# Wide self-attention: the next pair's scores directly behind the turns, ahead of reciprocals and values, and the probabilities copied ahead of the maxima

## The chip, the cores and the metric

The kernel runs on one NeuronCore of a Trainium2 chip. The time is the device time of one launch in microseconds (us). TensorE (PE in the rows) does the matmuls and transposes, VectorE (DVE), ScalarE (ACT) and GpSimd (POOL) the rest; PEld is the loading of TensorE's stationary operand. The engines run their own instruction lists in order and meet at semaphores.

## What is computed

The program is a decoder of six sub-layers on x of 16 batches x 256 rows x 128 columns. The change touches one of them, the self-attention of the second layer (16 heads of width 32), and only in the order of its instructions:

```python
def _mha(x, y, ...):                                  # here y = x, causal = True
    xn = _ln(x, lnx_g, lnx_b)
    yn = _ln(y, lny_g, lny_b)
    q = einsum('bsc,hcd->bhsd', xn, wq)
    k = einsum('btc,hcd->bhtd', yn, wk)
    v = einsum('btc,hcd->bhtd', yn, wv)
    a = softmax(einsum('bhsd,bhtd->bhst', q, k) * D ** (-0.5), axis=-1)
    a = a * mask                                      # masked after the softmax
    o = einsum('bhst,bhtd->bhsd', a, v)
    x_out = x + o.transpose(0, 2, 1, 3).reshape(...) @ li1_w + li1_b
```

## The kernel before

All stages run one after another. `attend_self` is called twice: with heads of width 8 (tiles `s2s_`) and with heads of width 32 (`WIDE`, tiles `s5a_`). It goes through 16 batches t of 8 steps p; a step handles a pair of heads. There is no scheduler and no pool: the order on every engine is the order in which the Python loops are written, and the semaphores only delay.

For a pair p of a batch, the work is a chain over three engines:

- TensorE `scores(p)`: q k^T into `scoreP[p % 2]` (L2269).
- VectorE `maxes(p)`: the row maxima, negated, into `nmax` (L2353).
- ScalarE `exps(p)`: four exponentials with row sums, into `prob[p % 2]` and `den` (L2181).
- TensorE `turn(p)`: six transposes of the probabilities into `probP` (L2279).
- VectorE `turn_out(p)`: mask and copy to `probT` (L2364).
- TensorE `pv(quad)`: after two pairs, probabilities times values into `oP` (L2299).

Between these go "items", all through one PSUM tile, `itemP`, which each must find free: `T` (transposed normalized rows, L2234), `Q0`, `Q1` (L2237), `K0`, `K1` (L2240) and `V0`, `V1` (L2244) of the projections, which ScalarE takes out; `R0`, `R1` (the transposed reciprocals of the softmax sums of the batch before, L2249) and `L` (its output projection, L2253), which VectorE takes out (L2385 for R, L2378 for L). TensorE's side of an item is called `make`, the other engine's side `take`. The tables say in which step an item is made: at place A `V0, V1, Q1, K1, L, T, Q0, K0` in steps 0 to 7, at place B `R0` in step 1 and `R1` in step 2. Since `itemP` is one tile, `make` waits for the `take` of the item before it: `Q1` for `R0`, `K1` for `R1`, and `T` for `L`:

```python
before = {"V0": [("K0", b + 1)], "V1": [("V0", b + 1)], "R0": [("V1", cap(b + 2)), ("L", b)],
          "Q1": [("R0", b), ("V1", b + 1)], "R1": [("Q1", cap(b + 2)), ("R0", b + 1)],
          "K1": [("R1", b), ("Q1", b + 1)], "L": [("K1", cap(b + 2)), ("R1", b + 1)],
          "T": [("L", b - 1), ("K1", b)], "Q0": [("T", b + 1)], "K0": [("Q0", b + 1)]}[n]
```

ScalarE takes a step's item ahead of that step's exponentials. `LEAD` is true in the narrow call only; there the scores of a pair already stand one step ahead.

Of the kernel before, what the change touches and what calls it, by code (L numbers as in the profile page):

```python
# [26 lines left out]
def wait(eng, sem, value):  # L27

    if isinstance(value, int) and value <= 0:
        return  # L30
    eng.wait_ge(sem, value)
# [1879 lines left out]
def attend_self(nc, ident, dram, tag, hat, base, dst, kind, D, ln, bias, src, affine=None, twice=False):  # L1911
# [6 lines left out]
    WIDE = D == 32  # L1918
# [10 lines left out]
    with ExitStack() as ctx:  # L1929
# [47 lines left out]
        def batches(eng):  # L1977
            for j in range(NB // 2):
                for s in range(2):
                    yield 2 * j + s, s  # L1980

        def first(t):
            return isinstance(t, int) and t == 0

        def last(t):
            return isinstance(t, int) and t == NB - 1
# [19 lines left out]
        LEAD = not WIDE  # L2006

        def following(t, s, p):
            if p + 1 < PAIRS:
                return t, s, p + 1  # L2010
            return None if last(t) else (t + 1, 1 - s, 0)

        def at(table, t, s, p, doing):
            for n, d in table.get(p, []):
                if (d < 0 and first(t)) or (d > 0 and last(t)):
                    continue
                doing(n, t + d, s if d == 0 else 1 - s)
# [9 lines left out]
        @block.sync  # L2027
        def _(sp):
            prep.load(sp)
            load_all(sp, S["loaded"], loads)  # L2030
# [184 lines left out]
        def _(pe):  # L2215
# [40 lines left out]
            def scores(t, s, p):  # L2256
                i = p % 2
                c = p // 2
                if p == 0:
                    pe.wait_ge(used["Q0"], t + 1)  # L2260
                    pe.wait_ge(used["K0"], t + 1)
                if p == 4:
                    pe.wait_ge(used["Q1"], t + 1)
                    pe.wait_ge(used["K1"], t + 1)
                wait(pe, S["maxed"] if kind == "causal" else S["exped"], t * PAIRS + p - 1)
                rows_of = lambda h: slice(64 * (p % 2) + 32 * h, 64 * (p % 2) + 32 * h + 32)
                for r, (a, b) in enumerate(CUTS):
                    for h in range(2):
                        ins = nc.tensor.matmul(scoreP[i][:, h, a:b], q[rows_of(h), c, r * P:r * P + P], k[rows_of(h), c, 0:b - a],  # L2269
                                               start=True, stop=True)  # L2270
                ins.then_inc(S["scores"], 1)

            def turn(t, s, p):
                i = p % 2
                pe.wait_ge(S["exped"], t * PAIRS + p + 1)
                wait(pe, S["probT_ready"], t * PAIRS + p)
                for h in range(2):
                    for m, a in enumerate(BLOCKS):
                        ins = nc.tensor.transpose(probP[:, h, m * P:m * P + P], prob[i][:, h, a:a + P], ident[:])  # L2279
                ins.then_inc(S["turned"], 1)  # L2280
# [29 lines left out]
            for n in ("T", "Q0", "K0", "V0") if LEAD else ("T", "Q0", "K0"):  # L2310
                if n != "T":
                    pe.wait_ge(used["T"], 1)
                make(n, 0, 0)
            if LEAD:
                scores(0, 0, 0)
            if bias:
                pe.wait_ge(S["bo_ready"], 1)
            for t, s in batches(pe):
                for p in range(PAIRS):
                    new = following(t, s, p) if LEAD else (t, s, p)  # L2320
                    if new:
                        scores(*new)
                    at(AT_A, t, s, p, make)
                    e = earlier(t, s, p, 1)
                    if e:
                        turn(*e)
                    at(AT_B, t, s, p, make)
                    e = earlier(t, s, p, 2)
                    if e and e[2] % 2 == 1:
                        pv(e[0], e[1], e[2] // 2)  # L2330
# [5 lines left out]
        @block.vector  # L2336
        def _(ve):
            st = Steps(ve, S["step"])
            st.begin(0)
            ve.wait_ge(S["masks"], 2)  # L2340

            def maxes(t, s, p):
                i = p % 2
                n = t * PAIRS + p
                ve.wait_ge(S["scores"], n + 1)
                wait(ve, S["exped"], n - 2 if kind == "causal" else n - 3)
                if kind == "causal":
                    for r, (a, b) in enumerate(CUTS):
                        for h in range(2):
                            ins = nc.vector.tensor_tensor_reduce(low[n % 3][:, h, a:b], scoreP[i][:, h, a:b], mask[:, a:b], -1.0, BIG, ALU.add,  # L2350
                                                                 ALU.min, nmax[:, p % 4, h, r:r + 1])
                else:
                    ins = nc.vector.tensor_reduce(nmax[:, p % 4, :, :].rearrange("p h r -> p (h r)"),  # L2353
                                                  scoreP[i][:].rearrange("p h (r k) -> p (h r) k", r=2), AX_X, ALU.max, negate=True)
                ins.then_inc(S["maxed"], 1)

            def turn_out(t, s, p):
                i = p % 4
                ve.wait_ge(S["turned"], t * PAIRS + p + 1)
                wait(ve, S["pv"], t * QUADS + p // 2 - 1)  # L2360
                if kind == "causal":
                    nc.vector.tensor_copy(probT[i][:], probP[:, :, 0:3 * P]).then_inc(S["probT_ready"], 1)  # L2362
                else:
                    nc.vector.tensor_tensor(probT[i][:], probP[:, :, 0:3 * P], mask[:].unsqueeze(1).to_broadcast([P, 2, 3 * P]),  # L2364
                                            ALU.mult).then_inc(S["probT_ready"], 1)

            def recip(t, s):
                ve.wait_ge(S["exped"], t * PAIRS + PAIRS)
                wait(ve, S["expanded"], t)
                nc.vector.reciprocal(rden[:], den[s][:]).then_inc(S["recip"], 1)  # L2370

            def take(n, b, s):
                if n not in ("L", "R0", "R1"):
                    return
                ve.wait_ge(made[n], b + 1)
                if n == "L":
                    ve.wait_ge(S["carried"], b + 1)
                    nc.vector.tensor_tensor(rows(dst, b), rows(dst, b), itemP[:, 0:TB * P].rearrange("p (g c) -> p g c", g=TB),  # L2378
                                            ALU.add).then_inc(used["L"], 1)
                    return  # L2380
                wait(ve, made["L"], b)
                half = int(n[1])
                ve.wait_ge(S["o_out"], b * 4 + 2 * half + 2 if WIDE else b + 1)
                w = 2 if WIDE else 1
                nc.vector.tensor_tensor(oT[:, w * half:w * half + w, :], oU[:, w * half:w * half + w, :],  # L2385
                                        itemP[:, 0:w * L].rearrange("p (c l) -> p c l", c=w), ALU.mult).then_inc(used[n], 1)

            if affine:
                prep.stats(ve, st, 0, 0)
            prep.stats(ve, st, 0, 1)  # L2390
            if affine:
                prep.stats(ve, st, 1, 0)
            ve.wait_ge(S["loaded"], LOADED)
            if bias:
                ve.wait_ge(S["values_out"], 1)
                nc.vector.tensor_tensor(bo[:], bo[:], oP[:, 0, 0:C], ALU.add).then_inc(S["bo_ready"], 1)
                ve.wait_ge(S["bo_ready"], 1)
            if LEAD:
                maxes(0, 0, 0)
            for t, s in batches(ve):  # L2400
                st.begin(t)
                for p in range(PAIRS):
                    new = following(t, s, p) if LEAD else (t, s, p)
                    if new:
                        maxes(*new)
                    if p == 0 and not first(t):
                        recip(t - 1, 1 - s)
                    e = earlier(t, s, p, 1)
                    if e:
                        turn_out(*e)  # L2410
                    at(AT_A, t, s, p, take)
                    at(AT_B, t, s, p, take)
                    if p == 0 and not last(t):
                        prep.stats(ve, st, t + 1, 1)
                    if p == 3 and affine and t + 2 < NB:
                        prep.stats(ve, st, t + 2, 0)
            turn_out(NB - 1, 1, PAIRS - 1)
            recip(NB - 1, 1)
            for n in (("R0", "R1", "L") if WIDE else ("R0", "L")):
                take(n, NB - 1, 1)  # L2420
            ve.wait_ge(used["L"], NB)
# [1543 lines left out]
```

## Time and profile before

| | |
|---|---|
| time before, median of 3 runs (lowest to highest) | 2798.28 us (2797.87 to 2806.37) |
| the profiled execution: its time, its span | 2795.5 us, 2793.8 us |
| mean granted TensorE clock over the span | 0.924 |
| busy over the span: PE, PEld, DVE, ACT, POOL | 86%, 64%, 72%, 59%, 40% |
| the changed stage (s5a) in the trace | scores from 1716.3 us, last probabilities at about 2160 us |
| scores(0) to scores(0) of the next batch | 27.51 us |

The profiled execution is one run, 2.8 us below the median. Its time is the span and 1.7 us around it. Shares of the whole span mix stages with different limits; for this change only the rows of the stretch 1716 to 2163 us count.

### The profile page before, as it was taken

What the parts mean: (1) busy time and instruction counts of PE and PEld (TensorE: products, weight loads), DVE (VectorE), ACT (ScalarE), POOL (GpSimd) and SP (SyncE); (2) the same over time, 40 slices, a digit from 0 to 9 for tenths busy, and PEclk for the clock granted to TensorE, in tenths of its full rate; (3) what the DMA queues carried; (4) which work ended last, traced back from release to release, by engine and by line L of the source; (5) the groups of instructions that cost most, each with busy time, mean ns of one, the idle gap of its engine ahead of it and who ended that gap; (6) DMA issues with size and microseconds to landing.
All of it is one profiled execution on the core that took longest, in us unless ns stands there. A gap on an engine that the chain in (4) does not pass through costs nothing. (4 is left out here: it accounts for less than half of the span.)

```text
span 2793.8 us, 48818 instructions
## 1 busy us (share of the span) xinstructions
PE 2405.5 (86%) x16107; PEld 1793.3 (64%) x16107; DVE 2002.1 (72%) x4456; ACT 1641.1 (59%) x4541; POOL 1108.5 (40%) x1577
## 2 busy tenths in 40 slices
PE   5888888887987999979974997999999789998696
PEld 4666666666974666656642774666666567765585
DVE  6999999996335777758979463777776557767565
ACT  6777767772225888866654344777776256654211
POOL 4455785865641111112321312222220155522774
PEclk7999999989997999999986998999999889999798
DMA  8500000004750000000004000000000000000376
GB/s 333 231 1 1 7 10 5 12 7 135 223 159 33 2 2 2 2 16 1 2 1 68 7 1 19 2 1 2 2 1 1 27 1 1 1 1 15 102 225 198
DMA packets 74187, 129.80 MB, mean 46 GB/s; under 512 B 29129, under 2 KB 47633, under 8 KB 69842
## 3 DMA queue, kind: packets, MB, share of 16 engines
q1 hardware_dynamic: 62418, 103.46, 12.3%
q0 software_dynamic: 9216, 19.02, 1.9%
q10 hardware_dynamic: 2304, 4.20, 0.4%
q8 instruction: 132, 2.16, 0.3%
q14 instruction: 117, 0.96, 0.1%
HBM read 69.23 MB, written 57.41 MB: 45 GB/s over the span
## 5 line engine op out<-in xcount | busy, mean ns | idle before, releaser
L1218 DVE TENSOR_TENSOR_SCAN s_state<-s_decay,s_state 128x4096 f32<-128x4096 f32 x32 | 279.0, 8718 | 1.6
L1090 PE MATMUL s_ysumP<-s_state,ident 128*128 128x256 f32 x1024 | 253.6, 395 | 0.0
L2181 ACT ACTIVATE s5a_prob<-s5a_scoreP,s5a_nmax 128x256 f32<-128x256 f32 x512 | 235.5, 481 | 22.7 <-DVE s5a_nmax L2353 21.0
L930 ACT ACTIVATE s_decay<-s_delta,s_aneg 128x255 f32<-128x255 f32 x512 | 211.8, 495 | 53.2 <-POOL s_delta L756 53.0
L2181 ACT ACTIVATE s2s_prob<-s2s_low,s2s_nmax 128x128 f32<-128x128 f32 (+1 forms) x512 | 225.4, 448 | 1.6 <-DVE s2s_nmax L2350 1.6
L1090 PEld LDWEIGHTS s_ysumP<-s_state,ident 128*128 128x128 f32 x1024 | 199.1, 201 | 27.6
L2353 DVE TENSOR_REDUCE s5a_nmax<-s5a_scoreP 128x4 f32<-128x1024 f32 x128 | 156.1, 1220 | 67.3 <-PE s5a_scoreP L2269 65.1
L2350 DVE CUSTOM_DVE_ANT_0 s2s_low<-s2s_scoreP,s2s_mask 128x128 f32<-128x128 f32 (+1 forms) x512 | 151.8, 353 | 55.6 <-PE s2s_scoreP L2269 54.3
L997 PE MATMUL s_bcP<-s_bc,s_sel 96*128 96x256 bf16 x768 | 131.6, 309 | 67.5 <-DVE s_state L1228 49.0
L2364 DVE TENSOR_TENSOR s5a_probT<-s5a_probP,s5a_mask 128x768 f32<-128x768 f32 x128 | 122.5, 957 | 63.1 <-PE s5a_probP L2279 62.0
L1228 DVE TENSOR_TENSOR s_state<-s_state,s_bcP 128x1024 f32<-128x1024 f32 x128 | 149.2, 1215 | 17.5 <-PE s_bcP L997 15.4
L1206 DVE TENSOR_TENSOR s_state<-s_bcP,s_du 128x1024 f32<-128x1024 f32 x128 | 146.6, 1213 | 10.6 <-POOL s_du L759 10.2
L997 PEld LDWEIGHTS s_bcP<-s_bc,s_sel 96*128 96x128 bf16 x768 | 78.6, 109 | 111.5 <-DVE s_state L1228 61.4
L2362 DVE COPY s2s_probT<-s2s_probP 128x768 f32<-128x768 f32 x128 | 122.3, 955 | 36.8 <-PE s2s_probP L2279 36.8
L2269 PE MATMUL s5a_scoreP<-s5a_k,s5a_q 32*128 32x256 f32 x1024 | 147.2, 405 | 0.8 <-ACT s5a_k L2160 0.8
L744 POOL TENSOR_TENSOR s_lost<-s_em,s_part 128x512 f32<-128x512 f32 x16 | 127.1, 7942 | 39.2 <-ACT s_part L910 39.2
L2269 PE MATMUL s2s_scoreP<-s2s_k,s2s_q 32*128 32x128 f32 (+1 forms) x1024 | 120.1, 356 | 4.8 <-issue 4.8
L2279 PE MATMUL s2s_probP<-ident,s2s_prob 128*128 128x128 f32 x768 | 110.1, 280 | 12.3 <-DVE s2s_probT L2362 5.9
L2279 PEld LDWEIGHTS s2s_probP<-ident,s2s_prob 128*128 128x128 f32 x768 | 87.7, 143 | 40.4 <-ACT s2s_prob L2181 31.8
L2279 PEld LDWEIGHTS s5a_probP<-ident,s5a_prob 128*128 128x128 f32 x768 | 89.4, 142 | 32.8 <-ACT s5a_prob L2181 19.8
L2181 ACT ACTIVATION_READ_ACCUMULATOR s5a_prob<-s5a_scoreP,s5a_nmax 128x1 f32 x512 | 110.2, 215 | 0.0
L2269 PEld LDWEIGHTS s5a_scoreP<-s5a_k,s5a_q 32*128 32x128 f32 x1024 | 88.7, 187 | 32.6 <-issue 26.1
(674 smaller groups left out, 6320.8 us busy)
## 6 DMA issues: line engine op xcount, KB each, us to landing
sorted<-blank SPq DMA_DIRECT2D x32, 1105.0 KB, 27.9
s_state<-in_m_w SPq DMA_DIRECT2D x40, 512.0 KB, 4.2
s5n_m_w<-in_m_w SPq DMA_DIRECT2D x40, 384.0 KB, 3.8
s_decay<-sorted SPq DMA_DIRECT2D x40, 130.0 KB, 2.6
s5n_m_xin<-sorted SPq DMA_DIRECT2D x40, 130.0 KB, 3.2
s4w_mats<-s_scratch SPq DMA_DIRECT2D x4, 1024.0 KB, 13.1
s_state<-parts SPq DMA_DIRECT2D x8, 256.0 KB, 6.7
s_state<-parts ACTq DMA_DIRECT2D x8, 256.0 KB, 7.1
```

The costliest lines, as they stand in the source:

```text
L744: st.do(nc.gpsimd.tensor_tensor(lost[:], em[:], part[:], ALU.subtract))
L930: ins = nc.scalar.activation(decay[c][:, n, 1:], delta[:, c, 1:], ACT.Exp, scale=aneg[:, c, n:n + 1])
L997: ins = nc.tensor.matmul(bcP[k % 2][:, n, :], sel[:, line + n, :], bc3[s][:], start=True, stop=True)
L1090: ins = nc.tensor.matmul(ysumP[:, c, :], ident[:], state[s][:, c, n, :], start=False, stop=(n == NS - 1))
L1206: ins = nc.vector.tensor_tensor(state[s][:, c, GN * g:GN * g + GN, :], bcP[g % 2][:], du[:, c:c + 1, :].to_broadcast([P, GN, L]), ALU.mult)
L1218: nc.vector.tensor_tensor_scan(cells, flat(decay[c]), cells, 0.0, ALU.mult, ALU.add).then_inc(S["scanned"], 1)
L1228: nc.vector.tensor_tensor(part, part, bcP[k % 2][:], ALU.mult).then_inc(S["bc_used"], 1)
L2181: ins = nc.scalar.activation(prob[i][:, h, a:b], (low[n % 3] if kind == "causal" else scoreP[i])[:, h, a:b], ACT.Exp, bias=nmax[:, p % 4, ...
L2269: ins = nc.tensor.matmul(scoreP[i][:, h, a:b], q[rows_of(h), c, r * P:r * P + P], k[rows_of(h), c, 0:b - a], start=True, stop=True)
L2279: ins = nc.tensor.transpose(probP[:, h, m * P:m * P + P], prob[i][:, h, a:a + P], ident[:])
L2350: ins = nc.vector.tensor_tensor_reduce(low[n % 3][:, h, a:b], scoreP[i][:, h, a:b], mask[:, a:b], -1.0, BIG, ALU.add, ALU.min, nmax[:, p % ...
L2353: ins = nc.vector.tensor_reduce(nmax[:, p % 4, :, :].rearrange("p h r -> p (h r)"), scoreP[i][:].rearrange("p h (r k) -> p (h r) k", r=2), ...
```

## The change

In the wide call alone, on TensorE `scores(p + 1)` is issued in step p directly behind `turn(p - 1)`; before, it was issued at the start of step p + 1, behind place B (`R0`, `R1`) and behind `pv`. On VectorE `maxes(p + 1)` is issued directly behind `turn_out(p - 1)`; before, it stood behind the takes of `R0`, `R1`, `L` and behind the statistics of the next batches. The first pair's scores and maxima are issued ahead of the loop. ScalarE's, GpSimd's and the DMA queues' lists are not changed, and the narrow call keeps its order. No instruction is added or removed.

```diff
@@ TensorE
-            if LEAD:
-                scores(0, 0, 0)
+            scores(0, 0, 0)
...
                 for p in range(PAIRS):
-                    new = following(t, s, p) if LEAD else (t, s, p)
-                    if new:
+                    new = following(t, s, p)
+                    if not WIDE and new:
                         scores(*new)
                     at(AT_A, t, s, p, make)
                     e = earlier(t, s, p, 1)
                     if e:
                         turn(*e)
+                    if WIDE and new:
+                        scores(*new)
                     at(AT_B, t, s, p, make)
@@ VectorE
-            if LEAD:
-                maxes(0, 0, 0)
+            maxes(0, 0, 0)
...
                 for p in range(PAIRS):
-                    new = following(t, s, p) if LEAD else (t, s, p)
-                    if new:
+                    new = following(t, s, p)
+                    if not WIDE and new:
                         maxes(*new)
                     if p == 0 and not first(t):
                         recip(t - 1, 1 - s)
                     e = earlier(t, s, p, 1)
                     if e:
                         turn_out(*e)
+                    if WIDE and new:
+                        maxes(*new)
                     at(AT_A, t, s, p, take)
                     at(AT_B, t, s, p, take)
```

The first place is on TensorE, in a batch from the second on, from `turn(0)` in step 1 to the item `K1` in step 3. Before (L2279 turn, L2249 R0 and R1, the two rows of L2299 one pv, L2269 scores, L2237 Q1, L2240 K1):

```order
L2279 MATMUL s5a_probP<-ident,s5a_prob 128x128 x6
L2249 MATMUL s5a_itemP<-ident,s5a_rdx 128x128 x4
L2299 MATMUL s5a_oP<-s5a_probT,s5a_v 32x256 x4
L2299 MATMUL s5a_oP<-s5a_probT,s5a_v 32x128 x4
L2269 MATMUL s5a_scoreP<-s5a_k,s5a_q 128x256 x4
L2237 MATMUL s5a_itemP<-s5a_xqT,s5a_wq 128x256 x2
L2279 MATMUL s5a_probP<-ident,s5a_prob 128x128 x6
L2249 MATMUL s5a_itemP<-ident,s5a_rdx 128x128 x4
L2269 MATMUL s5a_scoreP<-s5a_k,s5a_q 128x256 x4
L2240 MATMUL s5a_itemP<-s5a_xkT,s5a_wk 128x256 x2
```

Now, the same stretch of TensorE's list in the changed kernel:

```order
L2279 MATMUL s5a_probP<-ident,s5a_prob 128x128 x6
L2269 MATMUL s5a_scoreP<-s5a_k,s5a_q 128x256 x4
L2249 MATMUL s5a_itemP<-ident,s5a_rdx 128x128 x4
L2299 MATMUL s5a_oP<-s5a_probT,s5a_v 32x256 x4
L2299 MATMUL s5a_oP<-s5a_probT,s5a_v 32x128 x4
L2237 MATMUL s5a_itemP<-s5a_xqT,s5a_wq 128x256 x2
L2279 MATMUL s5a_probP<-ident,s5a_prob 128x128 x6
L2269 MATMUL s5a_scoreP<-s5a_k,s5a_q 128x256 x4
L2249 MATMUL s5a_itemP<-ident,s5a_rdx 128x128 x4
L2240 MATMUL s5a_itemP<-s5a_xkT,s5a_wk 128x256 x2
```

The scores moved ahead of `R0` and `pv`, and ahead of `R1`; nothing else moved, and each item still stands directly ahead of the next turn. So `R0` and `R1` now stand directly, or with one pv between, ahead of the item that waits for their take.

The second place is on VectorE, in the same batch, from `turn_out(0)` in step 1 to the take of `L` in step 4. Before (turn_out, take of R0, maxima; turn_out, take of R1, maxima; turn_out, statistics, maxima; turn_out, take of L):

```order
L2364 TENSOR_TENSOR s5a_probT<-s5a_probP,s5a_mask 128x768
L2385 TENSOR_TENSOR s5a_oT<-s5a_oU,s5a_itemP 128x512
L2353 TENSOR_REDUCE s5a_nmax<-s5a_scoreP 128x4
L2364 TENSOR_TENSOR s5a_probT<-s5a_probP,s5a_mask 128x768
L2385 TENSOR_TENSOR s5a_oT<-s5a_oU,s5a_itemP 128x512
L2353 TENSOR_REDUCE s5a_nmax<-s5a_scoreP 128x4
L2364 TENSOR_TENSOR s5a_probT<-s5a_probP,s5a_mask 128x768
L1858 BN_STATS s5a_n_stat<-xres 128x6 x2
L1861 BN_AGGR s5a_n_stat<-s5a_n_stat 128x2 x2
L2353 TENSOR_REDUCE s5a_nmax<-s5a_scoreP 128x4
L2364 TENSOR_TENSOR s5a_probT<-s5a_probP,s5a_mask 128x768
L2378 TENSOR_TENSOR s_xo<-s_xo,s5a_itemP 128x256
```

Now, from the maxima behind `turn_out(0)` on (the lines are one higher in the changed file):

```order
L2354 TENSOR_REDUCE s5a_nmax<-s5a_scoreP 128x4
L2386 TENSOR_TENSOR s5a_oT<-s5a_oU,s5a_itemP 128x512
L2365 TENSOR_TENSOR s5a_probT<-s5a_probP,s5a_mask 128x768
L2354 TENSOR_REDUCE s5a_nmax<-s5a_scoreP 128x4
L2386 TENSOR_TENSOR s5a_oT<-s5a_oU,s5a_itemP 128x512
L2365 TENSOR_TENSOR s5a_probT<-s5a_probP,s5a_mask 128x768
L2354 TENSOR_REDUCE s5a_nmax<-s5a_scoreP 128x4
L1858 BN_STATS s5a_n_stat<-xres 128x6 x2
L1861 BN_AGGR s5a_n_stat<-s5a_n_stat 128x2 x2
L2365 TENSOR_TENSOR s5a_probT<-s5a_probP,s5a_mask 128x768
L2354 TENSOR_REDUCE s5a_nmax<-s5a_scoreP 128x4
L2379 TENSOR_TENSOR s_xo<-s_xo,s5a_itemP 128x256
```

Each of the three takes (R0, R1, L) stood directly behind a turn_out and now stands behind the maxima of the pair after, which wait for that pair's scores.

## Rows read from the trace of the kernel before

**Rows 1.** Windows, whole stage and two batches: busy us by engine, then granted clock

```profile
core 0: us, PE busy (x) PEld busy (x) DVE busy (x) ACT busy (x) POOL busy (x), PEclk, DMA share, GB/s
...
1716.00:2163.00 447.00, 435.39 (x3523) 299.45 (x3524) 322.28 (x434) 348.49 (x1274) 108.27 (x247) 0.98 0.01 1
1806.00:1862.00 56.00, 55.23 (x463) 38.05 (x461) 41.59 (x58) 44.76 (x166) 15.55 (x36) 1.00 0.00 1
```

**Rows 2.** Timeline of PE, one batch: start us, length us, line, operation, count [idle before]

```profile
1914.83 0.82 PE L2279 MATMUL s5a_probP<-ident,s5a_prob 128*128 128x128 f32 x6
1915.68 0.66 PE L2249 MATMUL s5a_itemP<-ident,s5a_rdx 128*128 128x128 f32 x4
1916.27 0.86 PE L2299 MATMUL s5a_oP<-s5a_probT,s5a_v 128*32 128x256 f32 x16
1917.06 1.13 PE L2269 MATMUL s5a_scoreP<-s5a_k,s5a_q 32*128 32x256 f32 x8
1918.12 1.13 PE L2237 MATMUL s5a_itemP<-s5a_xqT,s5a_wq 128*128 128x256 f32 x4
1919.09 0.82 PE L2279 MATMUL s5a_probP<-ident,s5a_prob 128*128 128x128 f32 x6
...
1921.59 1.13 PE L2240 MATMUL s5a_itemP<-s5a_xkT,s5a_wk 128*128 128x256 f32 x4
...
1925.16 2.05 PE L2253 MATMUL s5a_itemP<-s5a_wo,s5a_oT 128*128 128x128 f32 x16
1927.04 0.82 PE L2279 MATMUL s5a_probP<-ident,s5a_prob 128*128 128x128 f32 x6
1927.79 1.13 PE L2269 MATMUL s5a_scoreP<-s5a_k,s5a_q 32*128 32x256 f32 x8
1929.24 0.44 PE L2234 MATMUL s5a_itemP<-ident,s5a_hs 128*128 128x128 f32 x2 [0.32 <-DVE s_xo L2378]
1929.51 0.82 PE L2279 MATMUL s5a_probP<-ident,s5a_prob 128*128 128x128 f32 x6
...
1942.34 0.82 PE L2279 MATMUL s5a_probP<-ident,s5a_prob 128*128 128x128 f32 x6
```

**Rows 3.** Timeline of DVE in the same batch

```profile
1911.21 1.22 DVE L2353 TENSOR_REDUCE s5a_nmax<-s5a_scoreP 128x4 f32<-128x1024 f32 x1 [0.90 <-PE s5a_scoreP L2269]
1912.35 0.34 DVE L2370 RECIPROCAL s5a_rden<-s5a_den 128x32 f32<-128x32 f32 x1
...
1918.23 1.22 DVE L2353 TENSOR_REDUCE s5a_nmax<-s5a_scoreP 128x4 f32<-128x1024 f32 x1 [1.00 <-PE s5a_scoreP L2269]
...
1920.82 0.68 DVE L2385 TENSOR_TENSOR s5a_oT<-s5a_oU,s5a_itemP 128x512 f32<-128x512 f32 x1
...
1928.78 0.41 DVE L2378 TENSOR_TENSOR s_xo<-s_xo,s5a_itemP 128x256 f32<-128x256 f32 x1
```

**Rows 4.** Timeline of ACT in the same batch: K1 taken, then exps(3)

```profile
1922.76 0.60 ACT L2160 ACTIVATE s5a_k<-s5a_itemP 128x512 f32<-128x512 f32 x1 [0.29 <-PE s5a_itemP L2240]
1923.25 0.47 ACT L2181 ACTIVATE s5a_prob<-s5a_scoreP,s5a_nmax 128x256 f32<-128x256 f32 x1
```

**Rows 5.** Waits in the whole stage: who for whom, us in total, times, longest

```profile
DVE s5a_nmax L2353 <- PE s5a_scoreP L2269: 65.1, 80, 11.8
...
PEld s5a_probP L2279 <- ACT s5a_prob L2181: 19.8, 35, 1.5
```

**Rows 6.** Windows of other stages with waits on PE; columns as in rows 1

```profile
1233.00:1241.00 8.00, 4.70 (x54) 2.95 (x52) 4.51 (x13) 3.15 (x13) 0.53 (x2) 1.00 0.00 0
1595.00:1607.00 12.00, 8.67 (x44) 7.57 (x45) 3.11 (x14) 2.14 (x4) 1.49 (x4) 0.58 0.01 1
653.00:662.00 9.00, 6.06 (x36) 5.14 (x36) 5.82 (x5) 1.37 (x5) 3.16 (x4) 1.00 0.33 96
```

**Rows 7.** Timeline of PE at the stage's start, at the low clock

```profile
1720.38 2.08 PE L2269 MATMUL s5a_scoreP<-s5a_k,s5a_q 32*128 32x256 f32 x8
```

**Rows 8.** Timeline of PE: the waits inside two windows of rows 6

```profile
1235.41 0.84 PE L2279 MATMUL s2s_probP<-ident,s2s_prob 128*128 128x128 f32 x6 [1.46 <-DVE s2s_probT L2362]
...
655.59 0.61 PE L997 MATMUL s_bcP<-s_bc,s_sel 96*128 96x256 bf16 x4 [2.42 <-DVE s_state L1228]
```

## The prediction

> **What bounds the stage now.** I first read the windows of the stage the change touches [rows 1]. TensorE is busy 435.4 of 447 us, and 55.2 of 56 us in two steady batches, at the full granted clock; the other engines stand at 82% or less. Busy spans of matmuls are modelled, so I did not trust that alone and read TensorE's timeline of one batch [rows 2], taking each group's start to the start of the next. The reader should see that these differences are the same wherever nothing waits: a turn 0.75 us (1927.04 to 1927.79), scores 1.06, an R item 0.59, a pv 0.79, a Q or K item 0.97 (V the same), L 1.88, T 0.27. Only a few gaps are longer: scores to T takes 1.45 instead of 1.06 because T waits for VectorE's take of L, and turn to R0 takes 0.85 instead of 0.75. A batch is 27.51 us (1914.83 to 1942.34). All its groups without waits make 8 x (0.75 + 1.06) + 4 x 0.79 + 6 x 0.97 + 2 x 0.59 + 1.88 + 0.27 = 26.8. So TensorE's list in its written order is full to within about 0.7 us a batch, and whatever is put on it as a wait is paid almost whole. Then I read the waits [rows 5]: VectorE waits 65 us for scores, but TensorE itself waits only 19.8 us, 35 times of 128, for exponentials. VectorE's idle time is not the stage's limit.
>
> **What the change can win.** It changes no duration and no count. The maxima of a pair come earlier by the pv and the R items that stood ahead of its scores. That helps ScalarE only where it waits for maxima; in seven of eight steps ScalarE first takes the step's item, which TensorE makes behind pv, R and scores in either order, so the item comes no earlier. The one step without such a take is that of L, step 4, and there turn(3) stands behind L's 1.88 us on TensorE anyway. The whole idle time of TensorE in the stage, 447 - 435.4 = 11.6 us [rows 1], caps the gain. I count nothing.
>
> **What it makes late.** Three takes on VectorE now stand behind maxima that wait for scores, and three items on TensorE wait for these takes. I work out each with the starts of [rows 2], the origin being the turn ahead. From [rows 3]: maxima start 1.17 after their scores start (1917.06 to 1918.23), I take 1.18; what follows them on VectorE starts 1.14 later (1911.21 to 1912.35). A take of R is 0.68 long and one of L 0.41, and T starts 0.05 behind the end of L's take (1928.78 + 0.41 = 1929.19, and 1929.24 [rows 2, 3]).
>
> Q1, behind R0. Before, turn(0) to Q1 is 1918.12 - 1914.83 = 3.29. Now scores at 0.75, R0 at 1.81, pv at 2.40, and TensorE is free for Q1 at 3.19. But maxima start at 0.75 + 1.18 = 1.93, the take at 3.07 (R0 is done by 2.5), its result is there at 3.07 + 0.68 + 0.05 = 3.80. Late by 0.51 against before.
>
> K1, behind R1, with no pv between. Before, turn(1) to K1 is 1921.59 - 1919.09 = 2.50. Now the same chain, scores 0.75, maxima 1.93, take 3.07, gives 3.80, where TensorE is free at 2.40. Late by 1.30. TensorE idles 1.40 here.
>
> L, behind K1. scores(4) needs ScalarE's take of K1: K1's make to take is 1.17 and the take 0.60 long [rows 2, 4], so with 0.05 on it the operand is there at 1.82 behind K1's start, and turn(2) and its 0.75 end at 1.72. Late by 0.10. K1 to L was 3.57 and becomes 0.97 + 0.85 + 1.06 + 0.79 = 3.67.
>
> T, behind L. Before, turn(3) to T is 1929.24 - 1927.04 = 2.20. Now maxima at 1.93, take of L at 3.07, T at 3.07 + 0.41 + 0.05 = 3.53. Late by 1.33, with TensorE idle for 1.72.
>
> In between nothing else is late. Step 2's and 3's exponentials wait for Q1 and K1, but they are done before their turns, since item, take and four exponentials are 1.17 + 0.49 + 4 x 0.47 = 3.5 [rows 2, 4], and from an item's start to the turn that needs these exponentials TensorE has a turn, scores and another item, 0.97 + 0.75 + 1.06 + 0.97 = 3.75 or more. The rest of the batch, from T to the next turn(0), has the same groups with scores and pv swapped, and costs the same. The statistics now stand behind maxima too; their GpSimd and ScalarE users come some 8 us later, so that hides them. The DMA queues are untouched. The first scores(0) moves only its place in the text.
>
> **The sum.** R0 and R1 exist in batches 1 to 15: 15 x (0.51 + 1.30 + 0.10) = 28.7. T waits for L in batches 1 to 14: 14 x 1.33 = 18.6. Together 47.3 us, 3.24 in a full batch, so 30.75 instead of 27.51. In the first batch, where no R and L exist, and in the last pairs, where no items stand, the earlier scores may win a microsecond or so, and the last batch may lose as much; I take 0 and 3 us either way. Against the profiled execution this is 2795.5 + 47.3 = 2842.8. The median of the runs is 2.8 above that execution, so 2845.6, and I say 2846.
>
> Bounds of the terms: with 1.22, the full length of the maxima, for 1.14, each of the three chains grows by 0.08, 3.5 us in all. Downwards, the T term rests on one hand-off; were it hidden by a take that starts as soon as the maxima's input is read, 18.6 would go: 2827. Q1's 0.51 is a difference of two near times and could be nothing (minus 7.7: 2838).
>
> **Rivals.** *TensorE's clock falls* in the new waits. Two idle times of 1.40 and 1.72 us a batch are new. In other stages the clock stayed at its full level, 2.4 GHz, in 1233 to 1241, with TensorE busy 4.7 of 8 us and a wait of 1.46, and in 653 to 662, with one of 2.42; in 1595 to 1607, where waits follow one another, the mean was 0.58 [rows 6, 8]. Here TensorE would stay near 90% busy. If it fell in each batch, the groups behind T (turn, scores, pv, 0.27 + 0.75 + 1.06 + 0.79 = 2.87 us) would run at 1.2 GHz, where a scores group is 2.08 instead of 1.13 long [rows 2, 7]: 2.6 us x 14 = 37 more, 2883. 7%. The Trainium skill (TensorE: Matmul & The Clock Gate, section "Why this matters for your kernels") advises to leave no idle gaps of more than about 3 us between bursts; by it the clock would stay up here, and the trace's 2.42 us case agrees.
>
> *The order of TensorE is not the limit (the other side).* Then the chain exponentials, turn, scores, maxima, exponentials of pair p + 2 binds, and the change takes four pvs and two R items out of it: 4 x 0.79 + 2 x 0.59 = 4.34 a batch, 15 batches, 65 us faster: 2733. For it speaks that VectorE waits 65 us for scores [rows 5]. Against it speak the start-to-start times, which leave 0.7 of 27.5 us. It decides only if groups without a named wait turn out to be stretched. The Trainium skill (Perfetto Trace Analysis, section "Identifying the Most-Contended Engine") says that matmul busy time misjudges TensorE and to go by the share of weight loading; that is 68% in the two batches [rows 1], and by it a third of TensorE would be free and this rival would hold. 1% for the full 65. A smaller form, that the takes are not late and only the waits shown go away, is capped at the 11.6 us of idle time: 2787. 3%.
>
> *The late items are hidden*: TensorE waits for the take, but what it did next had been waited for before. Then 2798. It needs exponentials as the last-ending wait of turns 1, 2 and 4, and they are so in only 35 of 128 turns [rows 5]. 3%.
>
> **How the numbers follow.** The forecast has 86%, its own range 2832 to 2858 from the bounds above. The clock has 7%, the two forms of faster 4%, no change 3%. For 8 in 10 I reach from 2827 (T's term gone) to 2868 (the clock down in some of the batches). 0.3% (8.4 us) is about what a measurement of this kernel tells from no change: slower 0.93, same 0.03, faster 0.04.
>
> **What would show it.** In the changed kernel: batches of 30.7 us from one turn(0) to the next; the makes of Q1 and K1 waiting for `s5a_oT` of VectorE, about 0.6 and 1.4 us, 15 times each; the make of T waiting for `s_xo` 1.7 us, 14 times; VectorE's waits for scores down from 65 us or moved; TensorE's busy share in steady batches near 90%; the clock at 1.00 throughout; start-to-start times of the groups unchanged. It is wrong if those takes start ahead of the maxima's end, if TensorE's groups shrink, or if the time moves outside the stretch of this stage.

## The result and the profile after

The changed kernel took 2867.87 us (median of 4 runs, 2864.03 to 2879.66) against 2801.01 us before (4 runs, one more than in the table of before): the ratio is 1.0244, with a 95% interval of 1.0208 to 1.0280. The forecast was slower, at 2846 us. The direction held and the size did not: the time is 67 us above before instead of 48. The ratio times the time before, 2869.4 us, is just past the upper end of the range, 2868.

The profiled execution after took 2870.27 us with a span of 2868.5, so 74.7 us more span than the one before. The first view is the windows of the stage, and of two single batches (busy us by engine, granted clock):

```profile
core 0: us, PE busy (x) PEld busy (x) DVE busy (x) ACT busy (x) POOL busy (x), PEclk, DMA share, GB/s
...
1716.00:2230.00 514.00, 457.74 (x3479) 313.77 (x3478) 319.51 (x430) 352.40 (x1265) 107.49 (x246) 0.94 0.00 1
...
1905.00:1939.00 34.00, 30.31 (x226) 20.85 (x222) 20.37 (x29) 22.37 (x80) 7.33 (x18) 0.90 0.00 1
2039.00:2070.00 31.00, 27.39 (x226) 19.04 (x224) 20.59 (x29) 22.15 (x80) 7.52 (x18) 1.00 0.01 1
```

TensorE was busy 55.2 of 56 us before [rows 1]; now it is busy 27.4 of 31 us where the clock holds (third row). The new thing is the second row: another batch, with the same instructions, takes 34 us at a mean clock of 0.90.

The second view is the waits in the stage (who for whom, us in total, times, longest):

```profile
DVE s5a_probT L2365 <- PE s5a_probP L2279: 162.9, 111, 3.5
...
DVE s5a_nmax L2354 <- PE s5a_scoreP L2269: 28.8, 34, 11.8
PEld s5a_itemP L2234 <- DVE s_xo L2379: 28.8, 14, 2.1
...
PE s5a_itemP L2234 <- DVE s_xo L2379: 23.2, 14, 1.7
...
PE s5a_itemP L2240 <- DVE s5a_oT L2386: 20.0, 15, 1.3
...
PEld s5a_probP L2279 <- ACT s5a_prob L2181: 16.0, 27, 1.6
...
PE s5a_itemP L2237 <- DVE s5a_oT L2386: 8.2, 15, 0.5
```

VectorE's waits for scores fell from 65.1 to 28.8 us [rows 5], and its waits for turns are 162.9 us now (62.0 before): its idle time moved, it did not go. TensorE's waits for exponentials hardly moved (19.8 to 16.0). In their place TensorE waits 14 times 1.65 us to make T, 15 times 1.33 us for K1 and 15 times 0.55 us for Q1, each for a VectorE take that now stands behind maxima.

The third view is TensorE's timeline. First a batch at the full clock, from turn(0) to K1 and, behind the mark, from L to T:

```profile
1923.27 0.82 PE L2279 MATMUL s5a_probP<-ident,s5a_prob 128*128 128x128 f32 x6
1924.02 1.13 PE L2269 MATMUL s5a_scoreP<-s5a_k,s5a_q 32*128 32x256 f32 x8
1925.08 0.66 PE L2249 MATMUL s5a_itemP<-ident,s5a_rdx 128*128 128x128 f32 x4
1925.67 0.86 PE L2299 MATMUL s5a_oP<-s5a_probT,s5a_v 128*32 128x256 f32 x16
1927.07 1.13 PE L2237 MATMUL s5a_itemP<-s5a_xqT,s5a_wq 128*128 128x256 f32 x4 [0.55 <-DVE s5a_oT L2386]
1928.04 0.82 PE L2279 MATMUL s5a_probP<-ident,s5a_prob 128*128 128x128 f32 x6
1928.79 1.13 PE L2269 MATMUL s5a_scoreP<-s5a_k,s5a_q 32*128 32x256 f32 x8
1929.85 0.66 PE L2249 MATMUL s5a_itemP<-ident,s5a_rdx 128*128 128x128 f32 x4
1931.84 1.13 PE L2240 MATMUL s5a_itemP<-s5a_xkT,s5a_wk 128*128 128x256 f32 x4 [1.33 <-DVE s5a_oT L2386]
...
1935.55 2.05 PE L2253 MATMUL s5a_itemP<-s5a_wo,s5a_oT 128*128 128x128 f32 x16
1937.44 0.82 PE L2279 MATMUL s5a_probP<-ident,s5a_prob 128*128 128x128 f32 x6
...
1940.98 0.44 PE L2234 MATMUL s5a_itemP<-ident,s5a_hs 128*128 128x128 f32 x2 [1.65 <-DVE s_xo L2379]
```

The starts are those worked out: turn(0) to Q1 is 1927.07 - 1923.27 = 3.80 us and turn(1) to K1 is 1931.84 - 1928.04 = 3.80, both forecast as 3.80; turn(3) to T is 1940.98 - 1937.44 = 3.54, forecast as 3.53. Now the part behind T, in a batch with the low clock (the first seven rows; the last of them is back at the full clock) and, behind the mark, in one without:

```profile
1906.96 0.44 PE L2234 MATMUL s5a_itemP<-ident,s5a_hs 128*128 128x128 f32 x2 [1.65 <-DVE s_xo L2379]
1907.23 1.04 PE L2279 MATMUL s5a_probP<-ident,s5a_prob 128*128 128x128 f32 x6
1908.20 2.08 PE L2269 MATMUL s5a_scoreP<-s5a_k,s5a_q 32*128 32x256 f32 x8
1910.21 1.51 PE L2299 MATMUL s5a_oP<-s5a_probT,s5a_v 128*32 128x256 f32 x16
1911.65 2.08 PE L2237 MATMUL s5a_itemP<-s5a_xqT,s5a_wq 128*128 128x256 f32 x4
1913.52 1.31 PE L2279 MATMUL s5a_probP<-ident,s5a_prob 128*128 128x128 f32 x6
1914.76 1.13 PE L2269 MATMUL s5a_scoreP<-s5a_k,s5a_q 32*128 32x256 f32 x8
...
2041.26 0.44 PE L2234 MATMUL s5a_itemP<-ident,s5a_hs 128*128 128x128 f32 x2 [1.65 <-DVE s_xo L2379]
2041.53 0.82 PE L2279 MATMUL s5a_probP<-ident,s5a_prob 128*128 128x128 f32 x6
2042.28 1.13 PE L2269 MATMUL s5a_scoreP<-s5a_k,s5a_q 32*128 32x256 f32 x8
2043.34 0.86 PE L2299 MATMUL s5a_oP<-s5a_probT,s5a_v 128*32 128x256 f32 x16
2044.13 1.13 PE L2237 MATMUL s5a_itemP<-s5a_xqT,s5a_wq 128*128 128x256 f32 x4
```

Both T wait 1.65 us. In the first batch the clock is down to 1.2 GHz some 1 us later: a scores group is 2.08 us long instead of 1.13, as at the stage's cold start [rows 7]. From T to Q0 it is 1911.65 - 1906.96 = 4.69 us against 2044.13 - 2041.26 = 2.87, and with Q0 and the next turn the batch loses 3.2 us.

The length of each batch, from one reciprocal of VectorE (L2370) to the next, all in the profiled executions:

| kernel | batches, us |
|---|---|
| before | 27.51 in 13 of 15, the last two 27.36 and 27.11 |
| changed | seven of 34.0, one of 32.3, then six of 30.8, the last 29.8 |

In the seven batches of 34.0 the clock falls behind T. In the one of 32.3 it holds behind T and falls behind K1, which waited 1.33 us, and it costs 1.5 us there:

```profile
1999.83 2.07 PE L2240 MATMUL s5a_itemP<-s5a_xkT,s5a_wk 128*128 128x256 f32 x4 [1.33 <-DVE s5a_oT L2386]
```

From the first to the last reciprocal it is 412.1 us before (1747.28 to 2159.42) and 485.0 after (1749.90 to 2234.92): 72.9 of the 74.7 us are in this stage. The rest is what lies ahead of it (2.6 later) and behind it (0.8 shorter).

### The profile page after: what moved, and what is told of

Its sections match the earlier page's. It is cut to its first block and busy times, and to the rows that moved or that the text cites. A ratio compares the mean times of both kernels' runs of the same rounds, so it can differ in the third digit from the quotient of the medians.

```text
span 2868.5 us, 48816 instructions
## 1 busy us (share of the span) xinstructions
PE 2431.8 (85%) x16105; PEld 1811.2 (63%) x16107; DVE 2004.6 (70%) x4456; ACT 1647.6 (57%) x4541; POOL 1112.1 (39%) x1577
## 5 line engine op out<-in xcount | busy, mean ns | idle before, releaser
L2365 DVE TENSOR_TENSOR s5a_probT<-s5a_probP,s5a_mask 128x768 f32<-128x768 f32 x128 | 122.1, 954 | 162.9 <-PE s5a_probP L2279 162.9
L2354 DVE TENSOR_REDUCE s5a_nmax<-s5a_scoreP 128x4 f32<-128x1024 f32 x128 | 156.7, 1225 | 38.3 <-PE s5a_scoreP L2269 28.8
L2269 PE MATMUL s5a_scoreP<-s5a_k,s5a_q 32*128 32x256 f32 x1024 | 153.8, 419 | 3.0 <-ACT s5a_k L2160 0.8
L744 POOL TENSOR_TENSOR s_lost<-s_em,s_part 128x512 f32<-128x512 f32 x16 | 112.6, 7036 | 40.2 <-ACT s_part L910 40.2
L2269 PE MATMUL s2s_scoreP<-s2s_k,s2s_q 32*128 32x128 f32 (+1 forms) x1024 | 118.8, 353 | 4.8 <-issue 4.8
L2279 PE MATMUL s2s_probP<-ident,s2s_prob 128*128 128x128 f32 x768 | 108.5, 278 | 11.3 <-DVE s2s_probT L2363 6.2
L2269 PEld LDWEIGHTS s5a_scoreP<-s5a_k,s5a_q 32*128 32x128 f32 x1024 | 94.1, 194 | 34.9 <-issue 26.2
L2279 PEld LDWEIGHTS s5a_probP<-ident,s5a_prob 128*128 128x128 f32 x768 | 94.9, 148 | 31.6 <-ACT s5a_prob L2181 16.0
L2279 PE MATMUL s5a_probP<-ident,s5a_prob 128*128 128x128 f32 x768 | 111.7, 284 | 2.7 <-ACT s5a_prob L2181 2.6
L2279 PEld LDWEIGHTS s2s_probP<-ident,s2s_prob 128*128 128x128 f32 x768 | 86.6, 142 | 39.2 <-ACT s2s_prob L2181 31.3
```

## The experiments

Two theories stood now. The first: the late takes through the one item tile cost what was worked out (47 us), and what goes beyond is TensorE's clock, which the new idle times let fall in some batches. The rival: the moved scores themselves, or something in the new order besides the takes, cost the rest. In each kernel below the edits are against the changed kernel or the one before, as said; ratios are to the kernel before.

**TensorE's part alone** (against the changed kernel, VectorE's list back as it was):

```diff
-            maxes(0, 0, 0)
+            if LEAD:
+                maxes(0, 0, 0)
...
-                    new = following(t, s, p)
-                    if not WIDE and new:
+                    new = following(t, s, p) if LEAD else (t, s, p)
+                    if new:
                         maxes(*new)
...
-                    if WIDE and new:
-                        maxes(*new)
```

> TensorE's part alone: scores(p + 1) directly behind turn(p - 1), VectorE's list as before. Takes stand directly behind turn_out again, so only R0 and R1, made 1.06 us later, are late. R1: turn(1), scores 0.75, R1 1.81, made 2.5, take 0.68, K1 at 3.3 instead of 2.50: +0.76 a batch, +0.10 for scores(4), nothing for Q1 and T. 15 x 0.86 = 13 us slower than before (ratio 1.0046), batches of 28.3 us. Theory (hand-offs through the one item tile, plus a clock that falls with the 1.7 us wait for L's take): the longest new wait is 0.9 us, so the clock stays at 1.00 through the stage. Rival (the scores' place itself, not VectorE's order, costs the time): most of the 70 us is here, batches over 32 us.

Measured: 1.0058 (1.0037 to 1.0078), 2818.4 against 2799.7 us. All batches but the last are 28.37 us, and the clock is 1.00 in the windows from 1800 to 2150 us. The moved scores cost 0.86 us a batch, as expected; K1 waits 0.8 us (11.7 us in 15), Q1's matmuls do not wait for the take (only the load of its weights does, 0.3 us). The rival that the place of the scores is the cost falls.

**VectorE's part alone** (against before: `maxes(*new)` behind `turn_out` and the first maxima ahead of the loop, TensorE's list as it was).

> VectorE's part alone: maxes(p + 1) ahead of the takes, but scores(p + 1) still behind R, pv. The takes of R0 and R1 then wait for scores that come later: Q1 5.28 behind turn(0) instead of 3.29 and K1 4.49 behind turn(1) instead of 2.50, +1.99 each, T +1.33. 15 x 3.98 + 14 x 1.33 = 78 us slower from hand-offs alone, batches of 32.8 us where the clock holds. With waits of 2.0, 2.0 and 1.7 us the theory expects the clock to fall in most batches, 3 us or more each time: 80 to 130 us slower in all. Rival (the order of the scores is the cost): near the time of before.

Measured: 1.0477 (1.0441 to 1.0512), 2931.9 us, 132 us slower. TensorE's waits:

```profile
PE s5a_itemP L2240 <- DVE s5a_oT L2385: 28.8, 15, 1.9
PE s5a_itemP L2237 <- DVE s5a_oT L2385: 28.8, 15, 1.9
...
PE s5a_itemP L2234 <- DVE s_xo L2378: 23.2, 14, 1.7
```

Q1 and K1 wait 1.9 us each, T 1.7. No batch reached the 32.8 us worked out for the full clock: they lie between 34.2 and 38.8, and the mean clock from 1800 to 2150 us is 0.88. So it is VectorE's half of the change that costs, and TensorE's half, costly alone, softens it (the maxima's input comes earlier). The 132 us are just past the upper end of what was expected, 130.

**L's take back ahead of the maxima** (against the changed kernel):

```diff
                     if e:
                         turn_out(*e)
+                    if WIDE:
+                        at(AT_A, t, s, p, take)
                     if WIDE and new:
                         maxes(*new)
-                    at(AT_A, t, s, p, take)
+                    if not WIDE:
+                        at(AT_A, t, s, p, take)
                     at(AT_B, t, s, p, take)
```

> The changed kernel with the take of L put back ahead of the maxima (R0 and R1 stay behind them). T's wait is back at about 0.3 us, Q1 +0.51, K1 +1.30 and scores(4) +0.10 stay: 15 x 1.91 = 29 us slower than before, batches of 29.4 us. If it is the wait for L that makes the clock fall, the clock stays at 1.00 and the time is 29 us above before (ratio 1.010). Rival: K1's wait of 1.33 us brings the clock down by itself or both together do; then some batches are 32.6 us and the time is 40 to 55 us above before.

Measured: 1.0197 (1.0144 to 1.0250), 2846.5 us in the median; the profiled execution's span is 2837.9. Batches are 29.48 us, the 29.4 expected, and five of 15 are 30.9. From the first to the last reciprocal it is 449.9 us, 37.7 more than before. Behind K1 in one of these five:

```profile
1793.46 1.93 PE L2240 MATMUL s5a_itemP<-s5a_xkT,s5a_wk 128*128 128x256 f32 x4 [1.33 <-DVE s5a_oT L2386]
1795.18 1.49 PE L2279 MATMUL s5a_probP<-ident,s5a_prob 128*128 128x128 f32 x6
1796.60 1.34 PE L2269 MATMUL s5a_scoreP<-s5a_k,s5a_q 32*128 32x256 f32 x8
```

Here it is K1's wait of 1.33 us that is followed by the low clock (1.93 us for a group of 1.13). So the clause "if it is the wait for L" was wrong as an only cause: a wait of 1.33 us does it too, in a third of the batches. It costs less than the rival's price, 1.45 us a batch instead of 3.2.

**R's takes back ahead of the maxima** (against the changed kernel; the same edit with `AT_B` in place of `AT_A`, L's take stays behind).

> The changed kernel with the takes of R0 and R1 put back ahead of the maxima (L stays behind them). K1 +0.76 and scores(4) +0.10 stay, T +1.33 stays: 15 x 0.86 + 14 x 1.33 = 31.5 us slower than before, batches of 29.7 us where the clock holds. If the wait of 1.66 us for L is what lets the clock fall, some batches are about 3.2 us longer with the low clock behind T, and the time is 35 to 75 us above before. Rival (it takes both long waits, K1's and T's, within ten microseconds): clock at 1.00 throughout and 31 us.

Measured: 1.0226 (1.0191 to 1.0262), 2860.8 us. Batches are 29.71 us, the 29.7 expected, in five of 14 full ones, and 32.8 to 32.9 in the other nine. From the first to the last reciprocal it is 473.2 us, 61 more than before. One long wait a batch is enough; both together are not needed.

**Filling TensorE's idle time ahead of T** (against the changed kernel; adds matmuls whose result nothing reads and leaves the order of everything else):

```diff
+    FILL = 10
...
             def make(n, b, s):
...
+                if WIDE and n == "T" and b > 1:
+                    pe.wait_ge(S["exped"], (b - 1) * PAIRS + 5)
+                    for _ in range(FILL):
+                        nc.tensor.transpose(scoreP[0][:, 0, 0:P], ident[:], ident[:])
                 for m, c in before:
                     wait(pe, used[m], c)
```

> The changed kernel with ten more transposes of the identity, 0.125 us each, put ahead of the make of T in batches 1 to 14, into the score tile that is free then: nothing reads them, and they fill 1.25 of the 1.66 us in which TensorE waited for the take of L. All hand-offs stay as late as they are. Theory (the idle time brings the clock down): no low clock behind T, every batch near 30.8 us unless K1's wait of 1.33 us, which stays, brings it down as in five batches of the run with L's take put back; 48 to 60 us slower than before instead of 70. Rival (the clock falls for another reason, or the late hand-offs alone make the 70 us): batches of 34 us stay, or the time grows by the transposes, 14 x 1.25 = 17 us.

Measured: 1.0201 (1.0146 to 1.0256), 2850.8 us. All 14 full batches are 30.82 us. The timeline of TensorE ahead of T, and the window of nearly the whole stage:

```profile
1928.25 1.31 PE L2233 MATMUL s5a_scoreP<-ident 128*128 128x128 f32 x10
1929.97 0.44 PE L2239 MATMUL s5a_itemP<-ident,s5a_hs 128*128 128x128 f32 x2 [0.41 <-DVE s_xo L2384]
1930.24 0.82 PE L2284 MATMUL s5a_probP<-ident,s5a_prob 128*128 128x128 f32 x6
```

```profile
1750.00:2200.00 450.00, 414.75 (x3374) 290.30 (x3370) 297.02 (x401) 322.09 (x1166) 100.04 (x229) 1.00 0.01 1
```

T starts when it did, relative to the batch, since L's take still ends late; only the idle time ahead of it is shorter, 0.41 instead of 1.65 us, and the low clock is gone. The order of all three engines, and every hand-off, is that of the changed kernel, TensorE has more work, and the stage is faster. First to last reciprocal takes 461.2 us (1754.91 to 2216.11). So of the 72.9 us, 461.2 - 412.1 = 49.1 are the hand-offs and 485.0 - 461.2 = 23.8 the clock. The table of batches gives the same without the filler: seven times 34.0 - 30.8 and once 32.3 - 30.8 make 23.9.

A rival is left: in the changed kernel six batches of 30.8 us went by without a fall although nothing filled T's wait, so one trace of the filled kernel could be luck. The runs speak against it. The five runs of the changed kernel took 2864.0 to 2880.7 us; of the eight of the two filled kernels, this one and the next, seven took 2844.0 to 2853.1 and one 2874.1. The kernel before stood at the same median beside both (2801.0 and 2801.1). The run of 2874.1 was not traced, and why it was long is open; one run of the kernel before in that series was 25 us above its median too.

**Filling ahead of K1 too** (the same with `n == "K1" and b > 0`, exponentials `b * PAIRS + 3`, five transposes).

> As before with five transposes more ahead of the make of K1. Theory: no low clock anywhere between the first and the last pairs, all batches within 0.1 us of 30.82, 14.5 x 3.31 = 48 us slower than before (ratio 1.017). Rival: some batches at 32 us or more, or at more than 31.2 because the fillers themselves delay K1 or T.

Measured: 1.0184 (1.0142 to 1.0226), 2851.6 us. All full batches are 30.81 us and the clock is 1.00. It adds nothing to the first filler: with that one alone K1 still waited 1.33 us and the clock did not fall there, though in the kernel with L's take put back it did in five batches.

**L's take ahead of the copy** (against before, a version aimed at beating both):

```diff
                     e = earlier(t, s, p, 1)
+                    if WIDE:
+                        at(AT_A, t, s, p, take)
                     if e:
                         turn_out(*e)
-                    at(AT_A, t, s, p, take)
+                    if not WIDE:
+                        at(AT_A, t, s, p, take)
```

> The kernel before with one thing moved: VectorE takes L ahead of turn_out(3) instead of behind it (L is made ahead of turn(3), so it is there first). The take then ends before T is issued, T's wait of 0.39 us goes and nothing new waits: batches of 27.1 instead of 27.51 us, 14 x 0.39 = 5.5 us faster (ratio 0.998), clock at 1.00. Rival (the take delays turn_out(3) and with it pv or the maxima of pair 5): no change or slower.

Measured: 0.9990 (0.9961 to 1.0019), 12 runs against 23: no difference that the runs can tell. In the trace it is there: batches are 27.17 us instead of 27.51, and 407.2 instead of 412.1 us from the first to the last reciprocal, 4.9 us against 5.5 expected.

**The same, with R0 made behind pv** (TensorE's `at(AT_B, ..., make)` moved behind `pv` in the wide call).

> As l_ahead_of_copy, and TensorE makes R0 behind pv instead of ahead of it in step 1, so that ScalarE's take of V1 is over when R0 is issued: 0.1 us a batch less, 7 us faster than before in all (ratio 0.9975). Rival (R0 is now too close to the scores and Q1, whose take waits): Q1 waits and batches are at 27.3 us or more.

Measured: 0.9988 (0.9967 to 1.0010). Batches are 27.07 us, the stage is 405.7 us, 6.4 less than before. Again the direction shows in the trace alone.

**The changed kernel and the one with L's take put back, once more.**

> The changed kernel once more, one look. Batches without a low clock are 30.82 us again and those with one 32 to 34. If where the clock falls depends on how the batches happen to lie in time, another number of batches than eight shows it, and the time differs from 2870 by some 3.2 us for each; if it depends on the order alone, again the first eight and the same time within a few us.

Measured: 2880.67 us, one run. Now nine batches are 34.0 us and one 32.2, then 30.8: ten batches with a low clock instead of eight, nine behind T and, in the one of 32.2, behind K1. The time is 10 us above the first profiled execution, 6.4 of them in this stage.

The falls do not come at random. The turn behind T, 0.82 us long at the full clock and 1.49 at the low one, has these lengths in batch after batch with a fall:

| execution | turn behind T, us |
|---|---|
| first | 1.47, 1.37, 1.26, 1.15, 1.04, 0.93, 0.82 |
| second | 1.49, 1.48, 1.48, 1.40, 1.30, 1.20, 1.09, 0.99, 0.89 |

A length of 1.49 means that the clock was low from the turn's start on; from there the low clock sets in about 0.1 us later behind T each time (in the first execution's seventh batch only with the scores behind the turn), then once behind K1, and then not at all. The second execution has more falls because it starts further back in this sequence.

> The kernel with L's take put back, once more, one look. 29.48 us a batch, or 30.9 with a low clock behind K1; by the chance theory another set of batches than the five of the first look (none to fifteen, 1.45 us each), by the rival the same five.

Measured: 2836.77 us, one run. The same five batches (the 2nd, 3rd, 7th, 11th and 12th) are 30.9 us. That is not the chance that I had expected. But it does not show that the order alone decides either: these two executions reached the first reciprocal within 0.6 us of each other (1752.14 and 1752.76), the two of the changed kernel 2.3 us apart.

## Why the prediction was right in direction and too small

Its steps, one by one:

- *TensorE's written order is the limit.* Right. Groups start to start did not change (0.75, 1.06, 0.79, 0.59), and every late item moved the batch by its lateness. The rival that the stage's chain of exponentials binds would have made the stage faster; it did not, though VectorE's waits for scores fell by 36 us. The rule from the Trainium skill (Perfetto Trace Analysis, section "Identifying the Most-Contended Engine"), to judge TensorE's headroom by the share of weight loading (and by its operations against the peak, which was not worked out here), would have called a third of it free. The trace disagrees: the groups without waits fill 26.8 of 27.51 us.
- *Hand-offs: 0.51, 1.30, 0.10 and 1.33 us a batch.* Right: measured 0.51 (3.80 - 3.29), 1.30 (3.80 - 2.50), 0.14 (K1 to L 1935.55 - 1931.84 = 3.71 against 3.57) and 1.34 (turn(3) to T 1940.98 - 1937.44 = 3.54 against 2.20). A batch is 30.82 us at the full clock, 30.75 were forecast. With the idle time filled the sum is 49.1 us, 47.3 were forecast. The single experiments separate it: TensorE's part alone costs 0.86 a batch, and putting back L's take or R's takes gives 29.48 and 29.71 us, as worked out.
- *The clock stays at 1.00.* This is the step that failed: the sum had nothing for the clock, and it measured 23.8 us. Its fall was a rival of 7%, argued down from single waits in other stages after which the clock had held [rows 6, 8]. In the changed kernel the clock fell behind T in seven of 14 batches in one execution and in nine in another, for 3.2 us each, and once in each behind K1, for 1.5 us. The mechanism and its price were in the text (2.6 us a batch, 2883 if in every batch); the chance was far too low, and the price a little, since the low clock also holds for Q0 and the next turn. That a filler of work without use takes these 24 us away shows the cause.
- *The range.* The upper end of the forecast's own range, 2858, does not follow from the bounds given: 2846 with 3.5 for the chains and 3 for the ends is 2852.5. It plays no part in the miss.

What stays open is why the clock falls in some batches and not in others with the same order. The batches with a fall come in regular patterns: with R's takes put back the lengths 32.9, 29.7 and 32.8 us come round every three batches, with VectorE's part alone 34.3, 34.2, 37.9, 38.8 and 35.7 every five, and in the changed kernel the fall slides by 0.1 us a batch until it is gone. That suggests that it matters when an idle time falls, and not only how long it is. No run here moves the stage in time, so this is not shown. The same wait of 1.33 us for K1 was followed by a low clock five times with L's take put back, once in each execution of the changed kernel, and never with T's idle time filled.

The Trainium skill (TensorE: Matmul & The Clock Gate, section "Why this matters for your kernels") warns of idle gaps of more than about 3 us. Here waits of 1.65 us and of 1.33 us were followed by the low clock, in between work that kept TensorE busy for some 88% of the batch. By that rule the clock would have held; the measurement decides.

## What to carry to other kernels

An instruction moved ahead on an engine that seems idle is paid for by what it is moved past: ask who waits for that, and whether the instruction itself waits. Here the maxima wait for scores 1.2 us away, and three short copies that free a tile shared by all items stood behind them; on a TensorE whose list is full each such microsecond is lost whole. And where a change puts repeated idle times of more than a microsecond on a TensorE that was full, count a fall of its clock as part of the likely case: a few rows in which the clock held after one such wait are samples, not a bound. If such a wait can't be removed, useless matmuls into a tile that is free may be worth adding; they took the falls away here, and the hand-offs still left the kernel some 50 us slower than before.

## What the runs showed of the hardware

- Waits of 0.8 us, 15 times in TensorE's part alone, left the clock at 1.00. Waits of 1.33 us were followed by 1.2 GHz in 5 of 15 batches with L's take put back and in 1 of 15 in each execution of the changed kernel; waits of 1.65 us in 7 and 9 of 14 there. A fall cost about 1.45 us behind K1 and 3.2 us behind T.
- Idle time can be dearer than work: ten added transposes in each of 14 batches (18 us of TensorE) made the stage 24 us shorter than in the changed kernel, trace against trace.
- What lies ahead of the stage is the same list of instructions in all kernels, and yet the stage's first scores start anywhere from 1715.9 to 1728.0 us over the twelve traces. So 5 us in a stage of this program can be read from a trace, but not from its time.
